# Loads of a pass move from SyncE to GpSimd in a four-layer Fourier kernel on one core

## The reference, cut to what matters

```
for i in range(4):
    x1 = fourier_layer(v)      # rfft2, 12 x 24 modes mixed by complex weights, irfft2
    x2 = einsum('bcxy,cd->bdxy', v, w_w[i]) + w_b[i]
    v = batch_norm(x1 + x2)    # statistics over images and positions
    if i < 3: v = relu(v)
out = einsum('bcxy,cu->bxyu', v, q_w) + q_b
```

## Time and profile before

| | us |
|---|---|
| median of 3 runs | 1394.54 |
| lowest, highest | 1385.4, 1395.76 |
| profiled execution, its own time | 1389.04 |
| span of the profiled execution | 1387.2 |
| PE busy | 1151.9 (83%) |
| DVE busy | 856.4 (62%) |
| ACT busy | 552.5 (40%) |
| POOL busy | 367.1 (26%) |

### The profile page before, as it was taken

The page is one execution under the profiler, slowest core; times in us unless marked ns, Lnnn a source line. Parts: engine busy times, 40 slices in busy tenths (PEclk is TensorE's granted clock), DMA queues, the critical chain, the costliest instruction groups (busy, mean ns, idle before and its releaser), DMA issues.

```text
span 1387.2 us, 40498 instructions
## 1 busy us (share of the span) xinstructions
PE 1151.9 (83%) x18183; PEld 660.6 (48%) x18183; DVE 856.4 (62%) x1033; ACT 552.5 (40%) x808; POOL 367.1 (26%) x525
## 2 busy tenths in 40 slices
PE   3659899999969879998996988998899777964696
PEld 3434555555534445555553445555455452323552
DVE  6546567777747566666664856665666561068664
ACT  2136444444446434444443644433344471100150
POOL 6394142021326340202122632220202251100000
PEclk9779799999989998999998999999999998976788
DMA  6269999798427999999962789999997176931001
GB/s 160 58 186 227 249 318 223 184 229 192 115 87 189 237 322 346 323 348 324 338 191 54 204 211 362 349 325 336 299 324 243 21 267 226 406 113 37 2 0 31
DMA packets 154711, 300.29 MB, mean 216 GB/s; under 512 B 32552, under 2 KB 98488, under 8 KB 137604
## 3 DMA queue, kind: packets, MB, share of 16 engines
q1 hardware_dynamic: 131418, 251.63, 59.9%
q0 software_dynamic: 20864, 45.32, 11.5%
q10 hardware_dynamic: 2256, 0.75, 0.2%
HBM read 147.86 MB, written 128.48 MB: 199 GB/s over the span
## 4 chain that ended last, share of the span: by engine, by line
PE 58%; DMA 13%; DVE 10%; ACT 5%; issue 5%; POOL 4%; SPq 3%; ACTq 0%; DVEq 0%; POOLq 0%
PE ps L1615 14%; PE ps L1654 12%; PE ps L1689 7%; PE ps L1677 7%; PE ps L1640 3%; PE ps L1578 3%; POOL arena L1249 2%; PE ps L1542 2%; DMA arena<-arena 2%; DMA inputs<-maps 2%; DMA maps<-arena 2%; DMA arena<-maps 2%; ACT arena L1426 1%; PE ps L1528 1%; PE ps L624 1%
## 5 line engine op out<-in xcount | busy, mean ns | idle before, releaser
L1094 POOL DMA_DIRECT2D arena<-arena x207 | 121.2, 593 | 556.2 <-ACT arena L1443 553.6
L1654 PEld LDWEIGHTS ps<-arena 48*128 48x128 f32 x3072 | 190.4, 197 | 90.4 <-issue 88.1
L1654 PE MATMUL ps<-arena 48*128 48x128 f32 x3072 | 210.9, 288 | 8.9 <-issue 7.3
L1426 ACT ACTIVATE arena<-ps,arena 128x1024 f32<-128x1024 f32 x96 | 112.3, 1202 | 226.9 <-PE ps L1654 202.0
L1435 ACT ACTIVATE ps<-ps 128x1024 f32<-128x1024 f32 x144 | 145.5, 1011 | 107.0 <-PE ps L1615 106.9
L2066 DVE STREAM_TRANSPOSE arena<-ps 128x1024 f32<-128x1024 f32 x96 | 177.1, 1928 | 2.2 <-PE ps L1677 2.2
L1615 PE MATMUL ps<-arena 32*32 32x512 f32 x2944 | 158.9, 639 | 10.8 <-DMA arena<-maps 7.9
L1677 PE MATMUL ps<-arena 32*32 32x512 f32 x3072 | 152.9, 608 | 6.0 <-DVE arena L2053 3.4
L2053 DVE STREAM_TRANSPOSE arena<-arena 128x2048 f32<-128x2048 f32 x64 | 144.2, 2285 | 22.1 <-issue 13.6
L1689 PE MATMUL ps<-arena 128*64 128x96 f32 x2304 | 125.6, 261 | 31.4 <-DVE arena L2066 28.1
L1689 PEld LDWEIGHTS ps<-arena 128*64 128x64 f32 x2304 | 106.2, 144 | 87.7 <-issue 49.6
(11 more groups left out here) (314 smaller groups left out, 1374.5 us busy)
## 6 DMA issues: line engine op xcount, KB each, us to landing
arena<-half_inverse SPq DMA_DIRECT2D x90, 384.0 KB, 10.8
half_inverse<-arena SPq DMA_DIRECT2D x120, 256.0 KB, 4.5
maps<-arena SPq DMA_DIRECT2D x112, 256.0 KB, 4.2
maps<-inputs SPq DMA_DIRECT2D x112, 256.0 KB, 11.4
arena<-maps SPq DMA_DIRECT2D x28, 1024.0 KB, 17.0
maps<-arena SPq DMA_DIRECT2D x28, 1024.0 KB, 11.5
inputs<-maps SPq DMA_DIRECT2D x28, 1024.0 KB, 15.3
arena<-in_mode_w POOLq DMA_DIRECT2D x48, 384.0 KB, 7.2
```

The costliest lines, as they stand in the source:

```text
L1094: eng.dma_start(dst, src).then_inc((modes_st[batch % 2], last_st, late_st)[part], 16)
L1426: nc.scalar.activation(half(h_out(l, q), h)[:, 1024 * pair:1024 * pair + 1024], ps[:, 2 * pair:2 * pair + 2, :].rearrange("p b n -> p (b n ...
L1654: last = nc.tensor.matmul(ps[:, b, at:at + 128], gtile[s][rows, 4 * b + 2 * h + n, :], iy[rows, :], start=False, stop=(i >= 2 and n == 1))
```

## The change

The loads of input maps and tiles are issued by GpSimd. Their waits are different: an input load of quad i+2 waits for `a_full` of quad i's set, that is for TensorE alone, and no longer for the relu and the store of quad i; the same holds for the tile of quad i+3. SP only stores, and it does not wait for the mix's last stores before its first one; GpSimd has taken these waits over. The six weights of the next layer are loaded and negated two at a time, at quads 1, 5 and 9, and not all at quad 0. A batch of four quads is placed at quads 4, 8 and 12 and after the loop, between the loads, in GpSimd's order.

```diff
@@ sync
-            def input_load(l, i, h):
-                sp.dma_start(half(h_in(l, i), h), maps_d[l - 1, ORDER[l][i], :, 2048 * h:2048 * h + 2048])\
-                  .then_inc(ld[i % 2][h], 16)
-
-            def g_load(l, i):
-                q = ORDER[l][i]
-                for t in range(2):
-                    sp.dma_start(gtile[i % 3][64 * t:64 * t + 4 * KY],
-                                 half_d[t, q].rearrange("y r g n -> (y r) g n"))\
-                      .then_inc(g_in[i % 3], 16)
...
                 store_inverse(sp, l, KYH - 2, 0)
                 store_inverse(sp, l, KYH - 1, 0)
-                sp.wait_ge(ix_st[1], half_stored(l, KYH - 2, 1))
-                sp.wait_ge(g_first[0], first_written(l, KYH - 2))
-                sp.wait_ge(ix_st[0], half_stored(l, KYH, 0))
-                sp.wait_ge(ix_st[2], half_stored(l, KYH - 1, 0))
-                sp.wait_ge(last_half, 64 * (l + 1))
-                g_load(l, 1)
-                sp.wait_ge(late_half[0], 64 * (l + 1))
-                sp.wait_ge(g_first[0], first_written(l, KYH))
-                g_load(l, 2)
...
-                sp.wait_ge(ix_st[3], half_stored(l, KYH - 1, 1))
-                for late in late_half:
-                    sp.wait_ge(late, 64 * (l + 1))
...
                         map_store(l, i, h)
-                        if l:
-                            input_load(l, i + 2, h)
-                    if i + 3 < QUADS:
-                        g_load(l, i + 3)
@@ gpsimd
+            def input_load(l, i, h):
+                pool.dma_start(half(h_in(l, i), h), maps_d[l - 1, ORDER[l][i], :, 2048 * h:2048 * h + 2048])\
+                    .then_inc(ld[i % 2][h], 16)
+
+            def g_load(l, i):
+                q = ORDER[l][i]
+                for t in range(2):
+                    pool.dma_start(gtile[i % 3][64 * t:64 * t + 4 * KY],
+                                   half_d[t, q].rearrange("y r g n -> (y r) g n"))\
+                        .then_inc(g_in[i % 3], 16)
...
                     for p in range(KYH):
                         first_tile(pool, l, p)
+                    pool.wait_ge(ix_st[1], half_stored(l, KYH - 2, 1))
+                    pool.wait_ge(g_first[0], first_written(l, KYH))
+                    pool.wait_ge(ix_st[0], half_stored(l, KYH, 0))
+                    pool.wait_ge(ix_st[2], half_stored(l, KYH - 1, 0))
                     pool.wait_ge(last_half, 64 * (l + 1))
+                    g_load(l, 1)
                     store_inverse(pool, l, KYH - 2, 1)
                     store_inverse(pool, l, KYH - 1, 1)
-                if l + 1 < LAYERS:
-
-                    pool.wait_ge(xs_ev, 2 * quad_of(l, 0) + 2)
-                    for ky in range(HELD):
-                        weights(l + 1, ky)
-                    for ky in range(HELD):
-                        negate(l + 1, ky)
-                    for batch in range(QUADS // 4):
-                        place(l, batch)
+                    pool.wait_ge(late_half[0], 64 * (l + 1))
+                    g_load(l, 2)
+                    pool.wait_ge(ix_st[3], half_stored(l, KYH - 1, 1))
+                    pool.wait_ge(late_half[1], 64 * (l + 1))
+                if l < PASSES:
+                    for parity in range(2):
+                        pool.wait_ge(map_st[parity], stores(l, 0))
+                    for i in range(QUADS - KEPT):
+                        for h in range(2 if l else 0):
+                            for pair in range(2):
+                                pool.wait_ge(a_full[pair], set_of(l, "out", i, h) + 1)
+                            input_load(l, i + 2, h)
+                        if i + 3 < QUADS:
+                            for pair in range(2):
+                                pool.wait_ge(a_full[pair], set_of(l, "out", i, 1) + 1)
+                            g_load(l, i + 3)
+                        if i % 4 == 1 and i // 4 < HELD // 2:
+                            ahead = (2 * (i // 4), 2 * (i // 4) + 1)
+                            for ky in ahead:
+                                weights(l + 1, ky)
+                            for ky in ahead:
+                                negate(l + 1, ky)
+                        if i % 4 == 0 and i:
+                            place(l, i // 4 - 1)
+                    place(l, LAST)
```

## The result

The changed kernel took 1398.13 us (median of 20 runs, 1388.3 to 1406.88), the kernel before 1387.05 in the same comparison (20 runs, 1376.06 to 1398.4). The ratio is 1.0106, 95% interval [1.0082, 1.0131]: slower by 1.1%, some 14.7 us (the two medians differ by 11.1), where I had forecast 7.7 us less. Two runs of the kernel before that lie over 1.5% above its fastest count as slow ones and are not in the ratio. The profiled execution's own time is 1395.45 us, its span 1393.4.

What follows compares the result with a forecast made beforehand. TensorE was taken to set pass 0's pace, with late loads, lower clock and issue waits adding excess in passes 1 and 2. Terms -20.2 + 7.5 + 5 = -7.7 us took 1394.5 to 1387, range 1364 to 1409.

Steps and rivals of the forecast that it cites:

- I take the 20.2 us as gained: Passes 1 and 2, nearly all before quad 3: late map loads and the lower clock behind them vanish, 20.2 us gained.
- the wait only moves to the next quad: Late loads in passes 1 and 2, other end of that term: the wait reappears one quad later, gain 0.
- the clock behind the waits: Passes 1 and 2: clock drops right behind long load waits, losing 5.1 and 3.4 us, counted within the 20.2.
- The start of a pass: First quads of each pass: tile, input load 2 and VectorE's first turn come later, costing 7.5 us, ends 0 and 18.
- Weights and negations: Quads 1, 5, 9: GpSimd's waits for weights delay later loads, costing 2.5 us twice, 5 in all, ends 0 and 39.
- C: Rival: GpSimd's order becomes the wait, 5 us lost at each of six negation stops, 1412 us; chance 0.21.
- Placing and stores: Quads 4, 8, 12 and SP's map stores: placing hidden, slower stores within 20 us of slack; 0, ends -5 and +5.
- B: Rival: two queues relieve the engines, half of issue waits and clock remainder goes, 19.9 us beyond the forecast, 1367; chance 0.25.
- D: Rival: DMA is the bound, issue order nothing; the 20.2 return later, start cost remains, about +3, 1397 us; chance 0.16.
- share 0.99 throughout: Sign of the DMA-bound rival: DMA share stays 0.99 throughout, with pass 1 within 3 us of 225.8.
- the 362 GB/s: Pass 1: rate needed to move 72.0 MB for 13 quads at 15.3 us a quad, against the pass's 319 GB/s.

Runs made afterwards that it cites:

- e1: Changed kernel with the tiles of quads 1 and 2 issued by SP again, GpSimd loading the rest; ratio 1.0137 to the kernel before.
- e2: Changed kernel with input load 2 (first half) issued ahead of the wait for late_half; ratio 1.0085 to the kernel before.
- e3: Changed kernel with each pair of weights negated two quads after its loads, at quads 3, 7, 11; ratio 1.0146 to the kernel before.
- e7: Changed kernel with GpSimd's input loads waiting for relu again, as SP's did; ratio 1.0104 to the kernel before.
- e8: Queues exchanged: SP loads early, GpSimd stores maps; weights in pairs, negated two quads later, input load 2 ahead of the mix's last stores; ratio 1.0056 to the kernel before.
- e18: Kernel before with early loads on SP's own queue ahead of the present quad's store, weights in pairs, input load 2 ahead of its wait; ratio 1.0045.
- e19: Changed kernel with 4 matmuls instead of 16 in each half of the 1x1 products, quads 2 to 15, passes 1 and 2; ratio 1.0040 to the kernel before.
- e16: Changed kernel profiled once more without an edit; span 1397.1 us.
- e5: Changed kernel with the map stores of passes 0 and 1 in pass 2's plain form, two 1 MB transfers in long runs; ratio 1.0120 to the kernel before.
- e17: Kernel before with 4 matmuls instead of 16 in each half of the 1x1 products, quads 2 to 15, passes 1 and 2; ratio 0.9858.
- e10: Kernel before with input loads of half the bytes, half of each input map not loaded; ratio 0.9914.
- e13: Kernel before with input loads, map stores and the stream behind the passes cut to 64 columns; ratio 0.9532.
- e14: Kernel before with input loads alone cut to 64 of 2048 columns, stores whole; ratio 0.9766.
- e12: Kernel before profiled once more without an edit; span 1379.6 us.
- e9: Kernel before with tiles alone loaded by GpSimd, weights and placings as in the changed kernel, input maps still on SP; ratio 1.0064.
- e11: Changed kernel with input loads of half the bytes, half of each input map not loaded; ratio 1.0044 to the kernel before.

## Why the prediction was wrong

**The step that failed is "I take the 20.2 us as gained"**, the late loads. I had written down the other end, 0, "the wait only moves to the next quad", and chose against it. The first half of the mechanism came true: map waits went from 11.7 us to 1.0 (14.9 to 4.3 in the second pair), and quad 3 of pass 1 follows quad 2 in 16.2 us instead of 24.3. But the rests together changed by -9.2 and +0.7 us in the two pairs of profiles. What stands in the place of the waits depends on the kernel: waits behind ScalarE, which waits for stores (4.2 to 16.8 us in the pass 1 rests of e1, e2, e3, e7, e8, e18 and e19, against at most 0.2 in the kernel before); "issue" waits (13.7 us in e16, 13.6 in e5); and, with "issue" gone, waits for transfers again (e17, e19). Taking a fifth of the bytes away (e10) left the rests as they were; only the kernels with hardly any input loads (e13, e14) shortened both of them much, by 20 to 31 us each against the earlier trace rows, or 13 at the least against e12. I had made 20.2 partly of the clock behind the waits; it falls just as well behind a wait for a store (e1: mean 0.93 in pass 1's rest).

**The start of a pass** was forecast at 7.5 us with ends 0 and 18, and measured 16.9 and 17.6. The mechanism is the one I named, mis-sized in the value. Of the 6.0 in pass 1, the tile takes 1.5 (forecast 1) and the input load 3.9 (forecast 1.5); in the second profile 1.9 and 0.9. In pass 2 the load costs 6.1 and 7.7. In pass 1 the load's transfer took 9.3 us as worked out (9.4), but it left 24.9 us into the pass and not 20.9. I had let the tile and GpSimd's eight stores drain at 350 GB/s and added 3 us for one store of SP's. But SP, freed from its own waits, issued its first map store at 476.12 instead of 485.36, and from 478 to 497 its queue moved 2.12 MB beside GpSimd's 3.18, at 280 GB/s together.

Two parts of the change meet there: the tile in front of GpSimd's eight stores, and SP's map stores set free early. e1 takes both back and its start of pass 1 is 30.0 us, with input load 2 still on GpSimd, so that queue alone doesn't make the load late. e8 and e18, which give the loads to SP, start at 30.0 too, and e9, with the maps' loads on SP and the tiles on GpSimd, keeps the cost. No run holds SP's stores back while GpSimd keeps the tiles, so the shares of the two parts are not shown. Pass 0's 3.8 and 3.3 us are partly the clock, which the sum left out: the start had a mean of 0.72 before and, after, 0.70 with a tile wait of 1.4 us, then 0.80 with 5.6. In e2, with 2.3 us of tile wait and 0.83, it is 30.6 us, as before.

The Trainium skill (DMA: Bandwidth & Descriptors, Specifications) gives about 1 us to the first byte of GpSimd's path. Here the issue at 477.36 had its first packet between 480 and 480.5, after 2.6 to 3.1 us, and the one at 833.40 in pass 2 between 834.8 and 835.4, after 1.4 to 2.0, where the tile landed in 5.5 us, like SP's 5.4. All lie above the page's figure, and the 4.1 of the earlier trace rows that I used as a fixed price is none.

**Weights and negations**, 5 us: nil (e3). GpSimd's stops of 18 to 25 us are longer than the 15 to 20 us of lead by which I judged C, and still TensorE doesn't wait for what stands behind them. e7 fits: a lead in loads that is worth nothing can be lost for nothing.

**Placing and stores**, 0 with ends of 5: placing held. Stores were the wrong zero: I had 20 us of slack for them, and in pass 1 they land 3.4 us later by the median and hold ScalarE up to 10.0 us. That is part of the substitution, since the time doesn't fall where they land sooner (9.2 us in e3, 11.4 in e5).

**The sum** was -20.2 + 7.5 + 5. The second pair of profiles gives +0.7 + 17.6 + 0, and a span 17.5 us longer; the timed ratio says 14.7 [11.4, 18.2]. These terms describe where the span lies longer; they are not prices that add. e9 has starts some 18 us longer than the kernel before, rests of passes 1 and 2 that are 12 to 19 us shorter together, and is slower by 0.64%, about 9 us. e1 has the starts back and is slower by 1.37%. So a late start is partly made up in the rest, and an early one partly lost there. The figure of 1387 us hides part of the miss: it began at the median of three runs, 7.5 us above that of twenty.

**The rivals.** B's gain didn't come: "issue" is 6.8 and 13.5 us in the rests (10.2 and 13.9 before), and in the second pair 13.7 and 14.2 (5.0 and 14.9 before). Its premise, instructions arriving late, holds, as the next paragraph shows. C has the right sign by the wrong mechanism (e3). D had the outcome: pass 1 within 1.8 us of 225.8, late loads' 20.2 given back, start cost remaining. Its +3 became +15 because it took over my start cost of 7.5 and a last fifth of the gain. Its reason is not shown: its sign "share 0.99 throughout" failed at 0.95 and 0.94, and e10 and e11 keep the rests with a fifth fewer bytes. The rule it named, that issuing from several engines brings no bandwidth (the Trainium skill, DMA: Bandwidth & Descriptors, Rules for kernel authors), is borne out by 311 and 308 GB/s after against 319 and 309, and by e19 against e17. It should have had a larger chance: the 362 GB/s that I worked out for a pass without excess is more than any rest here moved (338 at most, in e17).

**What "issue" is.** The traces show it, if one narrows the queue view in front of each such wait until it holds one packet of q8, the instruction queue. The longest of e16's pass 1, and the queue view of 589.5 to 590 us:

```profile
592.22 1.22 PE L1659 MATMUL ps<-arena 48*128 48x128 f32 x6 [3.59 <-issue]
...
q8 instruction: 1, 0.02, 14.8%
```

TensorE stood still from 588.6 on, the packet began at about 589.5, and work went on 2.7 us later. A rest of pass 1 or 2 has 31 or 32 such packets of 16 KB, one every 7 us. In both kernels' two profiles those eight rests have 77 "issue" waits of 0.3 us or more, and every one ended 2.3 to 3.4 us behind the start of a q8 packet, where about 15% would by chance. So TensorE waits for its instructions, which come through the same DMA engines as the maps. With fewer matmuls (e17) there are 27 packets and no such wait; with little traffic (e13) there are 31 and one wait of 0.2 us in pass 1.

**What stays open.** Why the fetch comes late isn't settled: e17 has the fullest DMA engines, 1.02, and not one "issue" wait. How the same execution time comes about through different waits isn't either: in e17 the DMA engines are full, in e10 and e11 (0.83 to 0.92) they are not, and e10's rests of 224.4 and 222.8 us are no shorter than e17's. And I can't split the 1.8% between e17 and e19 into the start (16.0 us of the spans' 23.4) and packet order with certainty, from one profile of each.

## What to carry to other kernels

Where a pass keeps shared DMA engines nearly full, a wait for a late load need not be time that asking earlier can win. Test it first by leaving the transfers out, and count the gain only if the whole stretch shortens, not if the wait disappears. For the same reason don't count a longer start as lost in full: look at what the rest of the pass gives back. Before moving transfers to another queue, look at what they will stand behind at the turn from one stage to the next, where there is no lead to hide it, at which waits the old queue loses with them, since its next transfers then go out earlier, and at the packet sizes of the two queues, since the smaller packets lose. One profile of a stretch that varies by 8 us between executions can carry a false gain: profile both kernels twice.

## What the runs showed of the hardware that was not expected

- Two queues that both had work moved equally many packets, not bytes: 667 to 668 packets but 4.58 to 1.22 MB in 20 us (e1); a store of 256 KB then took 25.8 us to land against a median of 11.6 before.
- TensorE's "issue" waits end with the fetching of instructions: all 77 of 0.3 us or more in eight rests ended 2.3 to 3.4 us behind the start of a q8 packet.
- They depend on the traffic and on the number of TensorE's instructions, but not on either alone: 13 quads at DMA share 0.99 and 1.00 had 10.2 and 5.0 us of them (before, e12), at 0.48 had 0.2 (e13), and at 1.02 with 628 fewer matmuls (3334 against 3962) none (e17).
- GpSimd's first packet came 1.4 to 4.1 us after the issue (pass 2 of the changed kernel; the earlier trace rows), so that a tile it issued landed after 5.5 us in pass 2 and 8.2 in pass 1.
- The rest of pass 2 in unchanged code took 231.9 and 223.8 us in two executions, and the 12 runs of e18 spread from 1374.23 to 1407.83.
